# A two-layer graph network: two output banks, a later address read, and one-hot rows written by ScalarE in layer 1

## What is computed

```python
h = relu(layernorm(x))
x = x + edge_mlp_and_node_mlp(h, edge_attr_64, src, dst)     # layer 0
h = relu(layernorm(x))
# layer 1: src and dst are edge_src and edge_dst of this function
logits = (data @ var_u)[edge_src] + (data @ -var_u)[edge_dst] + var_c   # 8 heads
q = softmax(logits, axis=-1)
x_sep = data[edge_dst] * edge_vals[:, None]
for m in range(8):
    y = y + segment_sum(q[:, m:m + 1] * x_sep, edge_src) @ var_w[m]
x = x + y + var_b
```

## Time and profile before

| | |
|---|---|
| median of 3 runs | 2352.28 us (2349.9 to 2352.87) |
| the profiled execution | 2348.29 us, span 2346.5 us |
| busy, share of the span | PE 71%, PEld 49%, DVE 61%, ACT 24%, POOL 69% |
| gathers of layer 0 start | 49 to 1089 us |
| gathers of layer 1 start | 1178 to 2316 us |
| granted TensorE clock, mean | 0.709 |

### The profile page before, as it was taken

One profiled execution on the slowest core, in us unless ns is written; L12 is line 12 of the kernel. 1 busy time (PEld: TensorE's weight loads), 2 busy tenths in 40 slices (PEclk: granted clock), 3 DMA queues, 4 the chain that ended last, 5 costly groups with the idle time before them and its releaser, 6 DMA issues.

```text
span 2346.5 us, 53388 instructions
## 1 busy us (share of the span) xinstructions
PE 1665.7 (71%) x9941; PEld 1160.7 (49%) x9941; DVE 1420.8 (61%) x6157; ACT 556.3 (24%) x1978; POOL 1622.2 (69%) x1700
## 2 busy tenths in 40 slices
PE   3888889998988999889745555555555655555555
PEld 2555555555555555555434444444444544444444
DVE  6344343444444444443268888888888888888885
ACT  2333333333333333333111111111111111111110
POOL 3777777777777777774467667676767676767673
PEclk8899898989899999999555555555555555555555
DMA  3544444444444444442243333333333333333332
GB/s 87 115 102 98 91 104 92 101 97 101 93 101 98 97 98 96 98 95 61 63 102 93 91 92 91 91 91 91 94 90 93 91 93 91 94 89 93 91 92 57
DMA packets 353332, 216.98 MB, mean 92 GB/s; under 512 B 284830, under 2 KB 325881, under 8 KB 353056
## 3 DMA queue, kind: packets, MB, share of 16 engines
q0 software_dynamic: 66800, 113.26, 21.1%
q1 hardware_dynamic: 284822, 102.20, 18.1%
q10 hardware_dynamic: 1684, 1.24, 0.2%
HBM read 209.80 MB, written 6.69 MB: 92 GB/s over the span
## 4 chain that ended last, share of the span: by engine, by line
DVE 29%; issue 26%; POOL 19%; PE 12%; DVEq 7%; DMA 6%; ACT 0%; POOLq 0%; SPq 0%; ACTq 0%
POOL X L583 18%; DVE EQW L1145 4%; DMA X<-table_src,slot_s 4%; DVE EQW L1151 3%; DVEq L1210 3%; DVE OT L995 2%; PE bank L1368 2%; DVE EX L1191 2%; DVE r L1183 2%; PE bank L1351 2%; DVE r L1187 2%; DVE r L1178 2%; DVE OE L1196 2%; PE bank L1377 2%; DVE sT L1212 2%
## 5 line engine op out<-in xcount | busy, mean ns | idle before, releaser
L591 POOL DMA_INDIRECT G<-table_node_and_list,slot_s x825 | 795.6, 964 | 374.5 <-issue 211.2
L583 POOL DMA_INDIRECT X<-table_src,slot_s x825 | 787.0, 954 | 288.9 <-issue 272.0
L1479 PE MATMUL bank<-Q,G 125*64 125x128 f32 x1650 | 416.6, 425 | 180.9 <-DVE Q L1204 180.9
L1479 PEld LDWEIGHTS bank<-Q,G 125*64 125x64 f32 x1650 | 314.8, 222 | 193.9 <-issue 125.0
L1009 DVE TENSOR_TENSOR sT<-sT,bank 65x16 f32 x275 | 46.2, 168 | 550.3 <-PE bank L1387 511.5
L1351 PE MATMUL bank<-filler 128*128 128x384 bf16 x1100 | 374.2, 340 | 2.4 <-issue 2.4
L1490 PE MATMUL bank<-R,w_z 65*64 65x64 f32 x1104 | 133.9, 316 | 279.1 <-DVE sT L1212 279.1
L995 DVE TENSOR_SCALAR OT<-KBT,base_p 48x375 bf16<-48x375 int32 x550 | 232.8, 424 | 68.7 <-issue 37.9
L1490 PEld LDWEIGHTS bank<-R,w_z 65*64 65x64 f32 x1104 | 122.9, 224 | 283.2 <-issue 283.2
L1368 PE MATMUL bank<-XT,w_ex 128*64 128x375 f32 x550 | 249.6, 537 | 4.7 <-issue 4.7
L1377 PEld LDWEIGHTS bank<-w,H 65*125 65x125 f32 x1650 | 230.2, 198 | 0.0
(11 more groups left out here) (165 smaller groups left out, 2006.9 us busy)
## 6 DMA issues: line engine op xcount, KB each, us to landing
KBT<-in_dst SPq DMA_DIRECT2D x550, 70.3 KB, 2.1
X<-in_edge_attr SPq DMA_DIRECT2D x275, 93.8 KB
HK<-keys SPq DMA_DIRECT2D x275, 93.8 KB
X<-table_src,slot_s POOLq DMA_INDIRECT x825
G<-table_node_and_list,slot_s POOLq DMA_INDIRECT x825
BW<-table_dst_parts SPq DMA_DIRECT2D x275, 6.0 KB
UW<-table_logit_src_parts SPq DMA_DIRECT2D x275, 0.8 KB, 1.6
table_node_and_list<-sm SPq DMA_DIRECT2D x1, 1562.5 KB
```

The source lines that it names most:

```text
L583: pool.indirect_dma_start(X[:, j, q, D:2 * D], None, tA, bass.IndirectOffsetOnAxis(ap=slot_s[:, j, q:q + 1], axis=0)).then_inc(gat_a[0][j] ...
L591: pool.indirect_dma_start(G[:, j, q, :], None, tH, bass.IndirectOffsetOnAxis(ap=slot_s[:, j, q:q + 1], axis=0)).then_inc(g_gather[j], 16)
L1479: last = pe.matmul(bank[2 + j % 2][0:D, 0:WM], G[0:P, j, q, 0:D], Q[:, j % 2, q].rearrange("p m n -> p (m n)"), start=(q == 0), stop=(q == ...
```

## The change

All of it is in layer 1.

- **Two banks.** The outputs of a turn go to bank 6 and bank 7 by turns. TensorE then waits for the adds of the turn before the last one, instead of the last one. The bank's number must be known when the code is written, so VectorE's and TensorE's loops take two turns (8 steps) a pass: `over_pairs` and `back_pair`.
- **Addresses.** The register load stands in a step of its own, `output_place`, behind `Q`; the add itself moves to the end of the step, behind "L less max".
- **One-hot rows.** ScalarE writes `OT` with two instructions, |base - receiver| into a new tile `OD` and relu(1 - OD) into `OT`, which is exact for whole numbers. They are for the group two ahead and stand at the end of ScalarE's step. The second waits for the first by a semaphore (u_D), and SyncE's reload of `KBT` waits for u_D instead of u_OT. VectorE's comparison stays in layer 0 alone.

```diff
@@ -167,6 +167,8 @@
         H1 = sb("H1", [DC, RB, GE])
         H2 = sb("H2", [P, RB, TG, DC])
         KBT = sb("KBT", [WP, RB, GE], I32)
+        OD = sb("OD", [WP, GE])
+        one_col = sb("one_col", [WP, 1])
         OT = sb("OT", [WP, RB, GE], BF16)
         BW = sb("BW", [WP, RB, D], BF16)
         OE = sb("OE", [P, RB, TG, WG])
...
@@ -356,6 +359,22 @@
             if not isinstance(t, int) or 0 <= RB * tk + jk < NG:
                 step(tk, jk)
 
+        def over_pairs(eng, body, depth):
+            for s in range(2 * RB):
+                body(s // RB, s % RB, s // RB % 2)
+            with eng.Fori(1, TURNS // 2) as i:
+                for u in range(2):
+                    for j in range(RB):
+                        body(2 * i + u, j, u)
+            for s in range(TURNS * RB, NG + depth):
+                body(s // RB, s % RB, s // RB % 2)
+
+        def back_pair(step, t, j, k, u):
+            jk = (j - k) % RB
+            dt = (j - k - jk) // RB
+            if not isinstance(t, int) or 0 <= RB * (t + dt) + jk < NG:
+                step(t + dt, jk, (u + dt) % 2)
+
         def done(eng, counter, t, j, k=0):
 
             g = RB * t + j - k
@@ -496,7 +515,7 @@
 
             def rows1w(t, j):
                 g = RB * t + j
-                done(sp, u_OT, t, j, RB)
+                done(sp, u_D, t, j, RB)
                 sp.sem_inc(sp_go, 1)
                 sp.dma_start(KBT[:, j, :], a["dst"][bass.ds(g * GE, GE)].partition_broadcast(WP)
                              ).then_inc(kbt_load[1][j], 16)
@@ -811,6 +830,17 @@
 
                 act.activation(EX[:, j], L[:, j], ACT.Exp).then_inc(u_EX, 1)
 
+            def window1_t(t, j):
+                act.wait_ge(kbt_load[1][j], (t + 1) * 16)
+                done(act, u_OT, t, j, 1)
+                act.activation(OD[:], KBT[:, j, :], ACT.Abs, bias=base_p[:, bass.ds(RB * t + j, 1)], scale=-1.0
+                               ).then_inc(u_D, 1)
+
+            def window1_one(t, j):
+                done(act, u_D, t, j)
+                done(act, u_U, t, j, RB)
+                act.activation(OT[:, j, :], OD[:], ACT.Relu, bias=one_col[:, 0:1], scale=-1.0).then_inc(u_OT, 1)
+
             def neighbours_w(t, j):
                 done(act, u_agg, t, j)
                 slots_w(1, t + 1, j)
@@ -821,9 +851,14 @@
             def body1w(t, j):
                 back(exps_w, t, j, 1)
                 back(neighbours_w, t, j, 2)
+                back(window1_t, t, j, -2)
+                back(window1_one, t, j, -2)
 
             for j in range(RB):
                 slots_w(1, 0, j)
+            for j in range(2):
+                window1_t(0, j)
+                window1_one(0, j)
             over_groups(act, body1w, DEPTH1)
 
             proof_ = load_proof(act)
...
@@ -989,11 +1025,11 @@
                 dve.tensor_copy(C[:, j], bank[6 + j % 2][0:P, 0:TG * DC].rearrange("p (q f) -> p q f", q=TG)
                                 ).then_inc(dve_g[0], 1)
 
-            def window_t(l, t, j):
-                dve.wait_ge(kbt_load[l][j], (t + 1) * 16)
-                done(dve, (f_h1, u_U)[l], t, j, RB)
+            def window_t(t, j):
+                dve.wait_ge(kbt_load[0][j], (t + 1) * 16)
+                done(dve, f_h1, t, j, RB)
                 dve.tensor_scalar(OT[:, j, :], KBT[:, j, :], base_p[:, bass.ds(RB * t + j, 1)], None,
-                                  ALU.is_equal).then_inc((f_OT, u_OT)[l], 1)
+                                  ALU.is_equal).then_inc(f_OT, 1)
 
             def window_e(t, j):
                 done(dve, f_seg, t, j, RB)
@@ -1021,7 +1057,7 @@
                 dve.tensor_reduce(pairs[:, bass.ds((RB * t + j) * TG, TG)], same[:, j % 2], AX_X, ALU.add)
 
             def body0w(t, j):
-                back(lambda t, j: window_t(0, t, j), t, j, 0)
+                back(window_t, t, j, 0)
                 back(same_next, t, j, 2)
                 back(window_e, t, j, 2)
                 back(count_same, t, j, 2)
@@ -1204,12 +1240,16 @@
                 dve.tensor_tensor(Q[:, j % 2], OE[:, j].unsqueeze(2).to_broadcast([P, TG, M, WG]),
                                   EX[:, j].unsqueeze(3).to_broadcast([P, TG, M, WG]), ALU.mult).then_inc(u_Q, 1)
 
-            def add_outputs(t, j):
+            place = {}
+
+            def output_place(t, j):
+                place["at"] = dve.value_load(first_of[0:1, bass.ds(RB * t + j, 1)], min_val=0, max_val=N - WG)
+
+            def add_outputs(t, j, u):
                 dve.wait_ge(u_y, t + 1)
                 done(dve, u_acc, t, j, 1)
-                first = dve.value_load(first_of[0:1, bass.ds(RB * t + j, 1)], min_val=0, max_val=N - WG)
-                to = yT[:, bass.ds(first, WG)]
-                dve.tensor_tensor(to, to, bank[6][0:D, j * WG:(j + 1) * WG], ALU.add).then_inc(u_acc, 1)
+                to = yT[:, bass.ds(place["at"], WG)]
+                dve.tensor_tensor(to, to, bank[6 + u][0:D, j * WG:(j + 1) * WG], ALU.add).then_inc(u_acc, 1)
 
             proofs = [0]
 
@@ -1219,26 +1259,26 @@
                 ins.then_inc(proof_dve, 1)
                 dve.wait_ge(proof_dve, proofs[0])
 
-            def body1w(t, j):
-
-                back(lambda t, j: window_t(1, t, j), t, j, 0)
+            def body1w(t, j, u):
+
                 back(window_places, t, j, 2)
-                back(add_outputs, t, j, 2 * RB)
                 back(exp_sums, t, j, 2)
                 back(denominators, t, j, 2)
                 back(inverses, t, j, 2)
                 back(edge_scales, t, j, 2)
                 back(head_weights, t, j, 2)
                 back(window_weights, t, j, 2)
+                back(output_place, t, j, 2 * RB)
                 back(reverse_edges, t, j, 1)
                 back(logits, t, j, 1)
                 back(reverse_weights, t, j, 1)
                 back(logits_max, t, j, 1)
                 back(reverse_sums, t, j, 1)
                 back(logits_less_max, t, j, 1)
+                back_pair(add_outputs, t, j, 2 * RB, u)
 
             dve.wait_ge(yT_zero, 1)
-            over_groups(dve, body1w, DEPTH1)
+            over_pairs(dve, body1w, DEPTH1)
 
 
             dve.wait_ge(u_found, NG)
@@ -1480,23 +1520,23 @@
                                      Q[:, j % 2, q].rearrange("p m n -> p (m n)"), start=(q == 0), stop=(q == TG - 1))
                 last.then_inc(u_agg, 1)
 
-            def outputs_w(t, j):
+            def outputs_w(t, j, u):
                 if j < RB - 1 and not (isinstance(t, int) and RB * t + j == NG - 1):
                     return
                 done(pe, u_R, t, j)
-                if not isinstance(t, int) or t > 0:
-                    pe.wait_ge(u_acc, RB * t)
+                if not isinstance(t, int) or t > 1:
+                    pe.wait_ge(u_acc, RB * (t - 1))
                 for m in range(M):
-                    last = pe.matmul(bank[6][0:D, 0:RB * WG], w_z[:, m, :], R[:, m].rearrange("c j n -> c (j n)"),
+                    last = pe.matmul(bank[6 + u][0:D, 0:RB * WG], w_z[:, m, :], R[:, m].rearrange("c j n -> c (j n)"),
                                      start=(m == 0), stop=(m == M - 1))
                 last.then_inc(u_y, 1)
 
-            def body1w(t, j):
+            def body1w(t, j, u):
                 back(logits_w, t, j, 0)
-                back(outputs_w, t, j, 3)
+                back_pair(outputs_w, t, j, 3, u)
                 back(aggregate_w, t, j, 2)
 
-            over_groups(pe, body1w, DEPTH1)
+            over_pairs(pe, body1w, DEPTH1)
 
             pe.wait_ge(proof_dve, 2)
             pe.matmul(bank[0][0:1, 0:2], ones[:, 0:1], proof[:, 0:2], start=True, stop=True).then_inc(proof_pe, 1)
```

More of the change, by code:

```diff
@@ L267, in build_gnn @@
                                     "scale", "head", "OH"))
+        u_D = sem("u_D")
         u_Q, u_agg, u_R, u_y, u_acc = (sem(f"u_{n}") for n in ("Q", "agg", "R", "y", "acc"))
@@ L879, in _ @@
             dve.memset(eps_col[:], EPS)
+            dve.memset(one_col[:], 1.0)
             dve.memset(no_key[:], -1.0)
```

## The result

| | before | forecast | after |
|---|---|---|---|
| median | 2351.18 us (4 runs) | 2274 | **2296.21 us** (4 runs, 2292.91 to 2299.81) |
| ratio to before | | | 0.9766, interval 0.9749 to 0.9783 |
| profiled execution, span | 2348.3, 2346.5 | | 2296.56, 2294.8 |
| a group in layer 1 | 4.147 us | 3.86 | 3.953 us |

The account below looks back on a forecast made before the run. VectorE's own instruction sequence bounds layer 1, with GpSimd's 3.774 us the next floor. -0.65 + 0.36 - 0.025 + 0.03 = -0.285 us a group, times 275 groups 78 us, gives a 2274 us median; range 2243 to 2325.

Parts of the forecast that it names:

- The first piece: VectorE's step from "L less max" to the next group's softmax sums: from 1.10 to 0.45 us, a gain of 0.65.
- the signs named beforehand: Group at 3.8 to 3.9 us; sums waiting for the exponential; stall ahead of EQW; TensorE's wait gone; GpSimd waiting less.
- The first rival: VectorE's load begins before Q and is hidden; GpSimd's gathers then bound at 3.774 us a group, 2249 us; chance 0.18.
- Q to EQW becomes 0.84: VectorE's step from the weights to the reverse edges, with the load there: 0.48 us becomes 0.84, a loss of 0.36.
- what is left stays as it is: VectorE's step from EQW to "L less max": 1.36 us, unchanged.
- the second: VectorE's step from sums to Q: 1.15 us, 1.35 behind the branch; loop terms 0.025 gained, 0.03 lost.
- the four pieces: VectorE's step cut at sums, Q, EQW and "L less max"; changes sum to -0.285 us a group.
- By itself it gives nothing: Two banks remove TensorE's 4.15 us wait a turn without gain alone, as VectorE didn't wait for TensorE.
- 0.025 us for the longer loop: VectorE's step behind the branch, 0.20 us longer, comes half as often: 0.025 us a group gained.
- ScalarE's rows cost nothing: Two more ScalarE activations, 0.99 us with hand-over, fit into 2.08 us of idle time before the next exponential.
- the nearest row: Profile row used to price ScalarE's new instructions: an activation over 64 x 375 takes 478 ns.
- no code is fetched anew: VectorE's longer loop isn't fetched again each pass; the rival that it is: about 2373 us, slower, chance 0.03.

Follow-up runs that it names:

- e1: The changed kernel with the address load moved from behind Q to directly ahead of the add, behind "L less max": 2268.15 us.
- e5: The whole change without its address part, the address read at the add as before; two banks, eight-group loops and ScalarE's rows stay: 2264.11 us.
- e2: The changed kernel with the address load behind Q done twice, the second value unused: 2466.13 us (one run).
- e8: The changed kernel without the run-time bounds check of the loaded address: 2251.21 us.
- e3: The kernel before with only the two banks and the eight-step loop added: 2313.8 us.
- e6: The kernel before with only the eight-step loops of VectorE and TensorE, one bank and the old wait: 2358.16 us.
- e4: The kernel before with only ScalarE's one-hot rows added, one bank, address read at the add: 2354.43 us.
- e10: The whole change with one bank and TensorE's old wait: 2627.73 us (one run).
- e11: The changed kernel with a third ScalarE activation over 375 columns, result unused, ahead of the two new ones: 2297.5 us.

## Why the prediction was right, and where it was not

**Right: VectorE's own sequence sets the pace, and the stall moves.** The first piece fell by 0.63 us (forecast 0.65) with the wait for the exponential in it (0.09 us a group, forecast 0.1 to 0.2), and the stall ahead of the add went to EQW. Of the signs named beforehand only the group's time, 3.8 to 3.9 us, was missed, by 0.05 us.

**Right: the load starts with Q, not before.** The first rival needed the sequencer to run ahead of Q. It doesn't: the load starts 0.10 to 0.14 us behind Q's start in every step. When it stands elsewhere, Q to EQW goes back to 0.48 us (e1) and 0.51 (e5), and a second load there is covered by nothing (e2).

**Wrong in size: "Q to EQW becomes 0.84".** It became 0.91, +0.42 us instead of +0.36. This term missed most: 0.06 x 275 = 17 us of the missing 23. In half of the steps the piece is 0.85 to 0.86, where the forecast had 0.83 without a second register instruction; in the other half 0.96 to 0.98. Three of these have one more register instruction ahead of EQW:

```profile
L1180 DVEq FUSED_REGOPS  x99: 53/57/57, 1213.7 to 2247.4; - x99
```

99 in 33 passes is three steps of eight, 0.11 us each with its gap: 0.04 us a group. The forecast had seen these three in the listing and given them 0.01. The fourth long step is the one behind the branch.

**Wrong: "what is left stays as it is".** EQW itself takes 375 ns on average instead of 350, and the piece 0.026 us more: 7 us. In e2 and e8 it takes 358 ns; why isn't settled. The first piece missed by 0.02 us (5 us), and the second came out 0.01 us shorter than before where the forecast had it 0.005 longer (4 us the other way). Together the four pieces give 53 of the 55 us measured.

**Wrong in its reasons: "By itself it gives nothing" of the two banks, and 0.025 us for the longer loop.** With each other they give 41 us (e3), alone the loop gives nothing (e6); the bank alone wasn't run. The forecast looked at one piece of the step behind the branch (0.20 us longer) when the whole step is 0.50 us longer; the rest sat in the mean of 1.10 and was booked as a gain of the one-hot row. The sum didn't suffer, since that piece went anyway; that is luck, and not the reasoning. And that VectorE didn't wait for TensorE held only, by the chain read in e6, while GpSimd had slack between them.

**Right: ScalarE's rows cost nothing, and the second bank is why.** e4 and e10 show what happens without it, and e11 how much room is left with it. Only the price was off: the nearest row, an activation over 375 columns at 478 ns, is not theirs:

```profile
L842 ACT ACTIVATE OT<-OD,one_col 48x375 bf16<-48x375 f32 x275 | 167.3, 608 | 29.5 <-ACT OD L836 12.4
L836 ACT ACTIVATE OD<-KBT,base_p 48x375 f32<-48x375 int32 x275 | 166.8, 607 | 18.3 <-DMA KBT<-in_dst 18.1
```

1.21 us of work instead of 0.96, harmless here since over 2 us were free.

**Right: no code is fetched anew.** The page's instruction queues, against 9 and 17 packets:

```profile
q8 instruction: 9, 0.15, 0.0%
q14 instruction: 18, 0.15, 0.0%
```

One packet more in all, for 33 passes of the loop (the forecast counted 34, and 68 for the loop of before, where the trace shows 66). The Trainium skill, page "Runtime: NRT & Kernel Launch", section "Instruction fetch mechanics", has a taken branch wait for a fetch when its target lies outside the two pages held. At eight groups a pass this trace shows no such fetch.

**What each part is worth** in this order, from the medians: banks and loop -41 us (e3), ScalarE's rows on top of them -50 (e5, where GpSimd has no slack left), the address part +32 (the change). The change measures -55 against its before, and the three add up to -59: the kernel before took 2351 to 2355 us beside the different runs. With the bounds left out another -45 (e8), down to GpSimd's pace.

## What to carry to other kernels

Before a register load is moved, look at what the instruction ahead of it waits for. In this kernel the sequencer ran ahead of one whose inputs were there, and much of the load was covered; behind one that waits on its neighbour the load started with it and showed. Cost a buffer's second copy by the chain of who waits for whom in both directions, and ask after every other gain whether the slack that hid a wait is still there: the loop (e6) and ScalarE's rows (e4) were worth nothing without the second bank. When a stall is register work, read what is in it; a fifth to a third of the 0.85 us between Q and EQW was a comparison with bounds.

## What was not expected of the hardware

Over 375 columns the two new activations, which read 48 partitions of SBUF, take 607 to 608 ns, integers or floats alike; the forecast's row, which reads 64 partitions of a PSUM bank, takes 478. The new ones also read their bias from a column (`base_p`, `one_col`), and that row doesn't. Which of these differences decides wasn't tried. An estimate points to the bias column: before the change the exponential, from SBUF and without such a column, takes 222 ns over 24 columns, and activations of one kind take 478 ns over 375 columns and 581 over 500, 0.82 ns a column. From SBUF without a bias column 375 columns would then take some 510 ns.

From Q's start to the next instruction that can start, a value load with its check takes 0.85 us; its load proper is 0.305 us of that, and leaving out the check took 0.18 to 0.28 us off "Q to EQW" in the three steps of eight that hardly wait for a gather.

And the step behind the branch of VectorE's loop was 0.5 us longer than the others before the change, although no code is fetched: most of it lies between `OE` and the add (0.78 us, 0.41 to 0.54 in the other steps) and behind the first sum (0.33 instead of 0.20). The trace has 22 register instructions of VectorE in that step and 12 to 14 in each of the other three.
